# Shares and normalisations of the slot stage moved from ScalarE to GpSimd

## The reference, cut to what matters

```python
slots = q_mu + exp(q_logsig) * noise
for _ in range(3):
    prev = slots
    q = _ln(slots, lnq_g, lnq_b) @ wq + bq
    logits = einsum('bnd,bkd->bnk', k, q) / scale
    attn = softmax(logits, axis=-1) + 1e-8
    attn = attn / sum(attn, axis=1, keepdims=True)
    slots = einsum('bnk,bnd->bkd', attn, v) @ wu + bu + prev
    h = _ln(slots, lnm_g, lnm_b) @ w1 + b1
    slots = gelu(h) @ w2 + b2 + slots
    slots = _ln(slots + x_cls[:, None, :], lnp_g, lnp_b)
```

## Time and profile before

| | |
|---|---|
| median of the runs | 892.08 us |
| the profiled execution | 893.99 us, its span from first to last instruction 892.1 us |
| busy over the span | PE 766.4 us (86%), DVE 568.9 (64%), ACT 529.1 (59%), POOL 364.6 (41%) |
| slot stage, 640 to 830 us | PE 125.18 of 190 us, DVE 150.91, ACT 127.67, POOL 66.40, granted PE clock 0.75 |

### The profile page before, as it was taken

The page is one execution under the profiler, slowest core; times in us unless marked ns, Lnnn a source line. Parts: engine busy times, 40 slices in busy tenths (PEclk is TensorE's granted clock), DMA queues, the critical chain, the costliest instruction groups (busy, mean ns, idle before and its releaser), DMA issues.

```text
span 892.1 us, 17850 instructions
## 1 busy us (share of the span) xinstructions
PE 766.4 (86%) x5685; PEld 640.3 (72%) x5685; DVE 568.9 (64%) x1970; ACT 529.1 (59%) x1144; POOL 364.6 (41%) x571
## 2 busy tenths in 40 slices
PE   5989799999999999999988978999948787862793
PEld 4766687788887888777767656999836565752793
DVE  1657877788686667777765663343499888885012
ACT  3654567676666766666665542333549888851472
POOL 1323544343342334233336653565542232327362
PEclk9999999999999999999998979999957979785797
DMA  9424404360710520120232024888520000001674
GB/s 249 125 76 132 165 1 148 97 224 1 240 59 24 164 82 1 53 53 7 71 134 63 28 79 145 243 253 247 166 80 1 1 1 0 1 1 49 165 208 131
DMA packets 82054, 88.52 MB, mean 99 GB/s; under 512 B 6155, under 2 KB 69851, under 8 KB 81323
## 3 DMA queue, kind: packets, MB, share of 16 engines
q1 hardware_dynamic: 78475, 80.19, 30.3%
q0 software_dynamic: 3488, 7.20, 2.2%
HBM read 69.03 MB, written 35.17 MB: 117 GB/s over the span
## 4 chain that ended last, share of the span: by engine, by line
PE 58%; DVE 20%; ACT 9%; issue 5%; POOL 4%; DMA 3%; SPq 1%; DVEq 0%; POOLq 0%; ACTq 0%
PE bank L713 6%; PE bank L1036 6%; PE bank L707 5%; PE bank L740 4%; DVE sb_smax L1542 4%; PE bank L780 3%; DVE sb_row_sum L1551 3%; PE bank L1044 3%; PE bank L845 3%; PE bank L749 2%; PE bank L1145 2%; PE bank L765 2%; PE bank L1153 2%; POOL sb_expd L2066 2%; PE bank L722 2%
## 5 line engine op out<-in xcount | busy, mean ns | idle before, releaser
L2066 POOL TENSOR_TENSOR sb_expd<-sb_expd,sb_rden 128x512 f32<-128x512 f32 (+1 forms) x128 | 111.3, 870 | 248.4 <-DVE sb_rden L1555 248.3
L1542 DVE TENSOR_REDUCE sb_smax<-bank 128x4 f32<-128x512 f32 (+1 forms) x128 | 74.2, 580 | 75.9 <-PE bank L740 40.4
L1273 ACT ACTIVATE sb_expd<-sb_shifted 128x512 f32<-128x512 f32 (+1 forms) x128 | 69.7, 545 | 42.6 <-DVE sb_shifted L1545 41.6
L2158 POOL TENSOR_TENSOR sb_rstd_all<-sb_rsq_all,sb_halves 128x4 f32<-128x4 f32 x44 | 45.0, 1023 | 108.8 <-DVE sb_rsq_all L1893 108.6
L1551 DVE TENSOR_REDUCE sb_row_sum<-sb_expd 128x4 f32<-128x512 f32 (+1 forms) x128 | 73.0, 570 | 7.7 <-ACT sb_expd L1273 7.6
L1545 DVE TENSOR_TENSOR sb_shifted<-bank,sb_smax 128x512 f32<-128x512 f32 (+1 forms) x128 | 75.0, 586 | 4.4
L707 PE MATMUL bank<-sb_h1T,sb_watt 128*128 128x128 f32 x512 | 70.5, 289 | 4.6 <-DMA sb_watt<-att_w 2.9
L707 PEld LDWEIGHTS bank<-sb_h1T,sb_watt 128*128 128x128 f32 x512 | 64.6, 202 | 7.3 <-DMA sb_watt<-att_w 3.3
L1036 PE MATMUL bank<-sb_blk_xT,sb_up_w 128*128 128x128 f32 x456 | 57.1, 275 | 0.0
L1036 PEld LDWEIGHTS bank<-sb_blk_xT,sb_up_w 128*128 128x128 f32 x456 | 54.0, 192 | 0.0
L1855 DVE TENSOR_TENSOR sb_hid<-bank,sb_hid 128x384 f32<-128x384 f32 x38 | 21.2, 558 | 51.1 <-ACT sb_hid L1321 51.1
(11 more groups left out here) (285 smaller groups left out, 1997.9 us busy)
## 6 DMA issues: line engine op xcount, KB each, us to landing
sb_up_w<-gate_up SPq DMA_DIRECT2D x38, 384.0 KB, 4.3
sb_v<-v_all SPq DMA_DIRECT2D x16, 576.0 KB, 6.6
rows_b<-pad_b SPq DMA_DIRECT2D x7, 1105.0 KB, 10.1
rows_a<-pad_a SPq DMA_DIRECT2D x7, 975.0 KB, 8.3
sb_up_w<-w1b SPq DMA_DIRECT2D x23, 256.0 KB, 3.7
v_all<-sb_moe_w SPq DMA_DIRECT2D x14, 308.0 KB
sb_blk_x<-rows_a SPq DMA_DIRECT2D x38, 65.0 KB, 3.2
sb_picked<-back_a SPq DMA_DIRECT2D x4, 512.0 KB, 5.5
```

What stands on the lines that cost most here:

```text
L1273: act.activation(exp_of(i, s, j), shifted[:, u % 2, :, 0:n], ACT.Exp, scale=DH ** -0.5).then_inc(exp_done, 1)
L1542: dve.tensor_reduce(smax[:, u % 2, :], s_in, X, ALU.max).then_inc(max_done, 1)
L2066: pool.tensor_tensor(e, e, rden[:, u % 2, :].unsqueeze(2).broadcast_to([P, QH, n]), ALU.mult).then_inc(norm_done, 1)
```

## The change

The shares and the two normalisations of each lane become GpSimd `tensor_scalar` instructions, four a step as before. A normalisation is now subtract the mean, then multiply by the root, both operands per partition; so `nbias` and the steps `shift_q` and `shift_m` of VectorE (28 instructions) go. The shares are multiply by the reciprocal, then add 1e-8. ScalarE loses 28 normalisations and 12 shares (160 instructions), GpSimd gains them. In the sorted order of GpSimd a normalisation stands directly behind its own root and waits on that root's semaphore.

```diff
-        "norm_q": (0.5900, 0.3921, 0.5369, 0.4138),
+        "norm_q": (-14.4877, -14.6377, -14.8345, -13.9260),
-        "shares": (2.2168, 1.9075, 1.0871, 1.5258),
+        "shares": (-12.7000, -13.5700, -13.0000, -13.2000),
-        "norm_m": (2.9165, 2.4781, 2.0449, 2.1655),
+        "norm_m": (-12.5585, -11.6081, -12.5116, -12.9450),
...
-            for step, it, g in slot_steps("norm_q", "scale_q", "exp", "shares", "norm_m", "scale_m", "gelu", "choice_exp"):
+            for step, it, g in slot_steps("scale_q", "exp", "scale_m", "gelu", "choice_exp"):
...
-            def shifted_by(it, g, k):
-                c = slice(4 * g, 4 * g + 4)
-                dve.wait_ge(root_ready[k], nth("root_" + k, it, g))
-                dve.scalar_tensor_tensor(nbias[:, c], mv_all[:, c, 0], -1.0, rstd_all[:, c], ALU.mult, ALU.mult).then_inc(
-                    shift_ready[k], 1)
...
+            def normed(it, g, k, src, dst):
+                pool.wait_ge(root_ready[k], nth("root_" + k, it, g))
+                for b in tiles(g):
+                    ins = pool.tensor_scalar(dst[:, b, 0:D], src[:, b, :], mv_all[:, b, 0:1], rstd_all[:, b:b + 1],
+                                             ALU.subtract, ALU.mult)
+                ins.then_inc(z_normed[k], 1)
+
+            for step, it, g in slot_steps("bias_u", "root_q", "shares", "root_m", "root_o", "send", "norm_q", "norm_m"):
+                if step == "shares":
+                    pool.wait_ge(rsum_ready, nth("share_sum", it, g))
+                    for b in tiles(g):
+                        ins = pool.tensor_scalar(att[:, b, :], att[:, b, :], rsum[0:C, b:b + 1], 1e-8, ALU.mult, ALU.add)
+                    ins.then_inc(att_ready, 1)
```

More of the change, by code:

```diff
@@ L492, in program @@
         var_ready, root_ready = ({k: sem(f"sl_{n}_{k}") for k in "qmo"} for n in ("var_ready", "root_ready"))
-        shift_ready, z_normed = ({k: sem(f"sl_{n}_{k}") for k in "qm"} for n in ("shift_ready", "z_normed"))
+        z_normed = {k: sem("sl_z_normed_" + k) for k in "qm"}
         zT_done, zT_ready = ({k: sem(f"sl_{n}_{k}") for k in "qm"} for n in ("zT_done", "zT_ready"))
@@ L1348, in _ @@
                 from_slot_bank(vu[:, 4 * g:4 * g + 4, 0:D], lambda t: quads(t)[0:C, :, :])
[L1352 to L1357, removed]
             def scaled(it, g, k, scale, bias):
@@ L1361, in scaled @@
                 act.activation(group_of(zsT, g), bank[2 * g][:, :], ACT.Identity, scale=scale, bias=bias).then_inc(zT_ready[k], 1)
-            for step, it, g in slot_steps("norm_q", "scale_q", "exp", "shares", "norm_m", "scale_m", "gelu", "choice_exp"):
-                if step == "norm_q":
-                    normed(it, g, "q", *((S, zs) if it < SLOT_ITERS else (x_sb, sent[0])))
+            for step, it, g in slot_steps("scale_q", "exp", "scale_m", "gelu", "choice_exp"):
                 if step == "scale_q" and it < SLOT_ITERS:
@@ L1376, in _ @@
                     ins.then_inc(att_exp, 1)
[L1377 to L1383, removed]
                 if step == "scale_m":
@@ L1893, in measured @@
                 dve.scalar_tensor_tensor(rsq_all[:, 0, c], mv_all[:, c, 1], 1.0, eps[:, c], ALU.mult, ALU.add).then_inc(var_ready[k], 1)
-            def shifted_by(it, g, k):
-                c = slice(4 * g, 4 * g + 4)
-                dve.wait_ge(root_ready[k], nth("root_" + k, it, g))
-                dve.scalar_tensor_tensor(nbias[:, c], mv_all[:, c, 0], -1.0, rstd_all[:, c], ALU.mult, ALU.mult).then_inc(
-                    shift_ready[k], 1)
             of_b = [routing("b", part) for part in range(len(PARTS["b"]))]
             dve.wait_ge(exp_out["a"], len(PARTS["a"]) + 1)
-            for step, it, g in slot_steps("add", "measure_q", "shift_q", "max", "share_sum", "updated", "measure_m", "shift_m",
+            for step, it, g in slot_steps("add", "measure_q", "max", "share_sum", "updated", "measure_m",
                                           "measure_o", "centre", "slots", "gated", "choose", "place"):
@@ L1916, in _ @@
                     measured(g, x_sb, "q")
-                if step == "shift_q":
-                    shifted_by(it, g, "q")
                 if step == "max":
@@ L1938, in _ @@
                     measured(g, S, "m")
-                if step == "shift_m":
-                    shifted_by(it, g, "m")
                 if step == "measure_o":
@@ L2158, in root @@
                 pool.tensor_tensor(rstd_all[:, c], rsq_all[:, 0, c], halves[:, c], ALU.pow).then_inc(root_ready[k], 1)
-            for step, it, g in slot_steps("bias_u", "root_q", "root_m", "root_o", "send"):
+            def normed(it, g, k, src, dst):
[10 more added lines that the diff above has]
+                    ins.then_inc(att_ready, 1)
                 if step == "bias_u":
@@ L2167, in _ @@
                     root("q", g, nth("measure_q", it, g))
+                if step == "norm_q":
+                    normed(it, g, "q", *((S, zs) if it < SLOT_ITERS else (x_sb, sent[0])))
+                if step == "norm_m":
+                    normed(it, g, "m", S, zs)
                 if step == "root_m":
```

## The result

The changed kernel takes **954.57 us**, the median of four runs (949.67 to 957.3); beside the kernel before on the same chip that is a ratio of 1.0697 (95% interval 1.0653 to 1.0741; one disturbed run of the kernel before is left out of it). The forecast was 904 with a range up to 917: the direction was right, the size was five times too small. The profiled executions stand 63.3 us apart (893.99 and 957.3), and their spans 63.4.

A forecast was written before the change was run, and what follows sets the result against it. ScalarE was taken to bound the stage, VectorE close behind. Start +4.7, C -2.5, D +4.9, E -1.1, A and B +5.6, end +0.4 gave 12.0 on 892.1: 904 us, range 890 to 917.

The forecast's parts named there:

- G: Price of one four-instruction step on GpSimd, normalisation or shares alike: 1.35 us, with ends 0.98 and 1.65.
- C: Period piece from slots(it-1,3) to the variance of measure_q(it+1,0): 16.33 us before, 15.3 forecast, leaving 0.75 of layer2's wait.
- the walk: The forecast's piece-by-piece count along VectorE's timeline, over periods, start and end, with G entering 23 times: +12.0 us.
- A: Period piece from measure_q(it,2) to the reciprocals of share_sum(it,1): 8.22 us before, 6.92 + 2G = 9.62 forecast.
- B: Period piece from the reciprocals of share_sum(it,1) to slots(it-1,3): 3.56 us before, 2.28 + 2G = 4.98 forecast.
- D: Period piece from the variance of measure_q(it+1,0) to updated(it,3): 3.71 us before, 2.44 + 2G = 5.14 forecast.
- E: Period piece from updated(it,3) to measure_q(it+1,2): 10.87 us before, 8.97 + G = 10.32 forecast.
- the start: Start of the slot stage, up to slots(-1,3): normalisations and biases ahead of roots and shares on GpSimd, +4.7 us.
- Rival 3: GpSimd instruction as dear as two-input addition, port takes 3 us, five updates at lower clock: 918 us, chance 0.18.
- The port: VectorE's instructions with two SBUF inputs wait for GpSimd's to end: nothing added, range carries up to 3 us.
- The first: ScalarE's freed 19.8 us shrink VectorE's idle time: faster below G = 0.82, 887 us at 0.6, chance 0.12.
- The second: GpSimd's instruction is as cheap as a copy: 895.5 us, 892 with TensorE at its higher clock, chance 0.20.

The follow-up runs named there:

- the copy: The changed kernel with the normalisation's GpSimd instruction replaced by a plain copy, order and waits kept: 901.68 us, ratio 1.0101.
- the mean added: The changed kernel with its normalisation's instruction as multiply by the root, then add the mean, places and waits kept: 912.59 us, ratio 1.0228.
- shares mid: Kernel before with only shares on GpSimd, shares(it,1) between root_m(it,0) and root_o(it-1,3), shares(0,0) ahead of lane 3's bias addition: 891.67 us, ratio 0.9993.

## Why the prediction was wrong

**The step that failed is the price of a step on GpSimd**: "neither row is clearly nearer, and I take the middle, G = 1.35 us, for normalisation and shares alike". The shares took 1.42; the normalisation took 3.14, nearly twice the upper end. That end came from an addition of two tensors, as if an instruction that reads one tensor could cost no more. A row of another operation bounds nothing, and "near 0.32 us from start to start" was 0.78 for the normalisation (0.35 for the shares). A second step failed with it: C had no term for GpSimd at all, and at this price GpSimd is what C waits for.

**What the walk makes of the right price.** Of the 23 places where G was counted, 14 are normalisations and 9 shares; 14 x 1.79 + 9 x 0.07 more than 12.0 gives +37.7. The other 25.7 of the 63.4 us are seen in the pieces. Those of one period:

| piece | predicted | its formula with 3.14 and 1.42 | measured |
|---|---|---|---|
| A | 9.62 | 11.48 | 12.42 |
| B | 4.98 | 6.84 | 6.85 |
| C | 15.3 | 15.3 | 19.25 |
| D | 5.14 | 7.00 | 7.98 |
| E | 10.32 | 12.11 | 13.80 |
| period | 45.4 | 52.7 | 60.30 |

Over the stage, counted as the forecast counted them, the three C lack 11.9 us, two E 3.4 and the last one, which the forecast left out, 3.4 up to slots(2,3); A, B and D lack 4.9 (of which 4.6 are five updates at the lower clock, see below), the start 2.5, and the end gives 0.4 back.

*C and E had a cover that the dearer step broke.* C was priced at what VectorE and layer2 fill, with no G in it. GpSimd's own chain in C is 1.33 to the sums, 1.51 for the shares, three times root and normalisation, 1.07 for root_o and 2.65 from there to the variance: 6.56 + 3 x (1.11 + N). At N = 1.35 that is 13.9 and hidden, as the forecast had it; at 1.74 it is 15.1 (measured 15.26), at 3.14 it is 19.3 (measured 19.25). The fixed parts are read from the changed kernel's own rows, so 3.14 fits by construction and 1.74 is the test; with the copy, C of this period is 14.58, just VectorE's own steps (14.56), so nothing came of the 0.75 us left for layer2. E likewise: norm_m(it,3) and norm_q(it+1,1) follow on each other, and the chain through both is 7.54 + 2N: 10.2 at 1.35 (under the forecast's 10.32), 11.0 at 1.74 (measured 10.97), 13.8 at 3.14. So the loss bends upwards, and a forecast that counts G a fixed number of times misses it.

*The lower clock of TensorE in A and D.* The update was taken at 1.24 us with its end, from the rows at the higher clock; at 2.09 us (739.02 to 741.11, granted clock 0.50, which is 1.2 GHz) it adds 0.92 in each, which is what the formulas of A (+0.94) and D (+0.98) lack. The kernel with the mean added has the update of A at two clocks, in successive periods (granted clock 0.92 and 0.64):

```profile
716.56 1.19 PE L1105 MATMUL bank<-sb_vu,sb_att_or_sent 77*128 77x129 f32 x8 [2.95 <-POOL sb_att_or_sent L2145]
764.87 1.68 PE L1105 MATMUL bank<-sb_vu,sb_att_or_sent 77*128 77x129 f32 x8 [2.91 <-POOL sb_att_or_sent L2145]
```

A took 10.10 us with the first and 10.59 with the second, where its formula gives 6.92 + 1.74 + 1.42 = 10.08: the difference is the update's own. Rival 3 had priced this, at 0.95 each (five of them are 4.75 us, where its sum has 4); the main sum had not. TensorE waited more after the change (granted clock 0.75 in the period, 0.84 before), but no run held the waits and changed the clock alone, so why it fell stays open.

**What held.** B's formula is exact once its prices are. The walk gave 899 for the copy (measured 901.68), and its pieces, corrected by those of the copy and of the change, gave 913 for the mean added (912.59). Piece D waited behind norm_q(it+1,0) as described, and the shares behind norm_q(it,2) in A. ScalarE came under 20 us. At the end the normalisation stood between root_q(3,3) and the sends: 4.48 us from that root to the next send, 1.24 before.

**The start** was forecast 4.7 us late at slots(-1,3) and came 14.5 late (690.67 against 676.20); with the measured prices its formula gives 4.7 + 4 x 1.79 + 2 x 0.07 = 12.0. What made the other 2.5 was not tested.

**The port** was given up to 3 us and cost less: VectorE's 181 instructions of a period took 35.26 us, where the 189 of before less eight L1898 (1.26) took 34.63, so 0.6 us a period, beside 31 us of new GpSimd work. The chance estimate had two-input instructions wait for half of GpSimd's; beside the normalisations the commonest of them, L1877, did not:

```profile
759.18 3.15 POOL L2137 TENSOR_SCALAR sb_z_all<-sb_S,sb_mv_all,sb_rstd_all 128x128 f32<-128x128 f32 x4
759.24 0.16 DVE L1877 SCALAR_TENSOR_TENSOR sb_rsq_all<-sb_mv_all,sb_eps 128x4 f32<-128x4 f32 x1
```

In the stage 19 of these L1877 overlap a normalisation's instruction, and 18 of them took their usual 0.16 us, one 0.20; the six that overlap an instruction of the shares took 0.25 to 0.32. The Trainium skill (SBUF — State Buffer, Who interferes with whom) says that a VectorE instruction with two SBUF inputs contends with a GpSimd instruction that reads SBUF, by an exclusive lock. By that rule an L1877 waits for the GpSimd instruction ahead of it to end. The bias addition of before held one up so (1.02 us), the normalisations here did not, and the measurement decides. No run here shows what sets the two apart.

**The rivals.** The first, ScalarE's relief wins, fell in every version, shares mid included. The second's 895.5 stood for the copy's price in both steps; with the copy in place of the normalisation alone it was 901.68. The shares at 0.98 too would take off 9 x 0.44 = 4.0 by the walk, an estimate of 898 that no run tested. The third had the right sign and the lower clock; its price for the normalisation was half of the real one, its 3 us for the port came to 0.6 a period, and it too had no GpSimd in C.

## What to carry to other kernels

Bound a price that the trace doesn't show by the same operation in the same form, not by a row with as many inputs; where there is none, the upper end is open and the range has to say so. Before a step is moved to an idle engine, write down that engine's order and add up, for each of its short steps that somebody waits for, what now stands ahead of it: the same 43 us of GpSimd work gave a period of 60.3 or 47.75 us. Note for each cover the price at which it breaks, since past that point the loss grows by more than the count of the sum.

## What the runs showed of the hardware

GpSimd's tensor_scalar on 128x128 costs by its pair of operations and by how many of its operands are per partition, and not by how many partitions it works on (subtract/multiply took 3.12 us on 77, 3.14 on 128). Four in a row took, in us:

| operations | two per-partition operands | one, and an immediate | two immediates | one operation alone, per-partition operand |
|---|---|---|---|---|
| multiply, add | 1.73 | 1.41 | 1.08 | |
| add, multiply | 1.74 | | | |
| multiply, multiply | 1.73 | | | |
| subtract, multiply | 3.14 | 2.80 | 2.48 | |
| multiply, subtract | 3.13 | | | |
| add, add | 3.13 | 2.79 | | |
| multiply | | | | 2.35 |
| subtract | | | | 2.34 |

One operation alone is dearer than multiply and add 0 (1.41). A copy took 0.99, and subtract/multiply on 64 columns instead of 128 took 2.24 in place of 3.14. The Trainium skill (GPSIMD Engine Reference, Engine selection) calls one-input work on GpSimd roughly line-rate. No run here shows that rate itself; beside GpSimd's own copy (0.99) multiply/add with two immediates stays near (1.08), and the pair that this change used takes three times as long. Why the pairs differ no run here shows.
